# Attention in a macaron block: one exponential per head, and the products with V of two key tiles in a row

## The reference

```
q = (x @ wq.T).reshape(B, S, 16, 16)      # B = 4, S = 2048
k = (x @ wk.T).reshape(B, S, 4, 16)       # 4 key heads, each used by 4 query heads
v = (x @ wv.T).reshape(B, S, 4, 16)
attn = einsum('bqhd,bkhd->bhqk', q, k) / 4
attn = where(causal, attn, -inf)
attn = softmax(attn, axis=-1)
out = einsum('bhqk,bkhd->bqhd', attn, v)
```

## Time and profile before

| | us |
|---|---|
| median of 3 runs (9195.44 to 9199.81) | 9198.21 |
| profiled execution, its own time | 9194.41 |
| its span | 9192.7 |
| exponentials of attention, first start (first call) to last start (second call) | 276.9 to 8605.8 |
| PE busy over the span | 8340.8 (91%) |
| DVE busy | 7658.0 (83%) |
| ACT busy | 4879.4 (53%) |

### The profile page before, as it was taken

One profiled execution on the slowest core, in us unless ns is written; L12 is line 12 of the kernel. 1 busy time (PEld: TensorE's weight loads), 2 busy tenths in 40 slices (PEclk: granted clock), 3 DMA queues, 4 the chain that ended last, 5 costly groups with the idle time before them and its releaser, 6 DMA issues. The chain is left out here.

```text
span 9192.7 us, 130248 instructions
## 1 busy us (share of the span) xinstructions
PE 8340.8 (91%) x35938; PEld 3452.2 (38%) x35938; DVE 7658.0 (83%) x10977; ACT 4879.4 (53%) x7770; POOL 3581.8 (39%) x1746
## 2 busy tenths in 40 slices
PE   7999999999998888888878888888679999999999
PEld 3333333345543333333333333333533333333455
DVE  7888888876666999999979999999278888888666
ACT  3566666642234666665655555555026666666421
POOL 0001000000005999999969999999000000000000
PEclk8899999999999999999989999999879999999999
DMA  6111211122152222222223222222660211111221
GB/s 173 24 25 26 34 25 25 25 51 64 53 192 92 73 68 67 69 66 68 67 88 94 85 87 84 84 87 85 198 156 17 32 26 25 25 25 25 60 64 46
DMA packets 569122, 615.81 MB, mean 67 GB/s; under 512 B 204225, under 2 KB 374209, under 8 KB 568481
## 3 DMA queue, kind: packets, MB, share of 16 engines
q1 hardware_dynamic: 568480, 608.05, 24.7%
HBM read 434.15 MB, written 172.15 MB: 66 GB/s over the span
## 5 line engine op out<-in xcount | busy, mean ns | idle before, releaser
L740 DVE TENSOR_REDUCE ffn_att_mx<-psum 128x1 f32<-128x512 f32 (+3 forms) x4708 | 2909.1, 668 | 541.8 <-PE psum L573 298.7
L697 ACT ACTIVATE ffn_att_e<-psum 128x1024 f32<-128x1024 f32 (+3 forms) x2560 | 2180.8, 895 | 1161.3 <-PE psum L633 1155.7
L570 PE MATMUL psum<-ffn_att_k,ffn_att_q 96*128 96x512 bf16 (+3 forms) x5388 | 1845.1, 361 | 81.0 <-DMA ffn_att_v<-v 76.7
L537 POOL TENSOR_SCALAR_AFFINE_SELECT ffn_att_e<-ffn_att_e 128x512 f32<-128x512 f32 x512 | 324.8, 634 | 3234.6 <-ACT ffn_att_e L697 3234.6
L633 PE MATMUL psum<-ffn_att_q,ffn_att_k 99*128 99x512 bf16 (+3 forms) x5120 | 1500.4, 349 | 27.2 <-issue 26.3
L1517 POOL TENSOR_TENSOR scan_r_h<-scan_r_h,scan_r_cs 128x1024 f32<-128x1024 f32 x512 | 1195.3, 2357 | 202.4 <-ACT scan_r_state L1678 199.1
L1517 POOL TENSOR_TENSOR scan_f_h<-scan_f_h,scan_f_cs 128x1024 f32<-128x1024 f32 x512 | 1193.7, 2357 | 178.9 <-ACT scan_f_state L1678 175.8
L600 PE MATMUL psum<-ffn_att_e,ffn_att_v 128*32 128x512 f32 (+3 forms) x10240 | 1204.0, 542 | 5.1 <-ACT ffn_att_o L716 4.3
L1596 PE MATMUL psum<-scan_f_h,ident 128*128 128x512 f32 x2048 | 1035.0, 647 | 138.6 <-POOL scan_f_h L1517 138.4
L1596 PE MATMUL psum<-scan_r_h,ident 128*128 128x512 f32 x2048 | 997.1, 629 | 126.8 <-POOL scan_r_h L1517 126.0
L570 PEld LDWEIGHTS psum<-ffn_att_k,ffn_att_q 96*128 96x128 bf16 x5388 | 522.0, 98 | 1419.0 <-DVE ffn_att_mx L740 991.1
(11 more groups left out here) (211 smaller groups left out, 8673.6 us busy)
## 6 DMA issues: line engine op xcount, KB each, us to landing
scan_f_cs<-scan_f_bcd SPq DMA_DIRECT2D x264, 256.0 KB, 3.4
scan_r_cs<-scan_r_bcd SPq DMA_DIRECT2D x264, 256.0 KB, 3.4
ffn_att_q<-q_parts SPq DMA_DIRECT2D x72, 384.0 KB, 6.4
q_parts<-ffn_in_q SPq DMA_DIRECT2D x192, 128.0 KB
scan_f_win<-xp SPq DMA_DIRECT2D x18, 1036.0 KB, 7.2
scan_r_win<-xp SPq DMA_DIRECT2D x18, 1036.0 KB, 7.2
ffn_att_q<-q_parts SPq DMA_DIRECT2D x72, 256.0 KB, 8.0
mamba_out_ys<-yz SPq DMA_DIRECT2D x18, 1024.0 KB, 7.0
```

Of the source, the lines that this page charges most:

```text
L570: ins = nc.tensor.matmul(at, q[0:PARTS, i // HALF, h, i % HALF * P:(i % HALF + 1) * P], k[0:PARTS, c * P:c * P + w], start=True, stop=not ...
L697: nc.scalar.activation(E[:, s % PB, 2 * hp:2 * hp + 2, off:CH], psum[:, 2 * hp:2 * hp + 2, off:CH], ACT.Exp, scale=HD ** -0.5).then_inc(e_ ...
L740: nc.vector.reduce_max(mx[:, heads[0]:heads[-1] + 1, i // HALF, i % HALF, c // TT], psum[:, turn, 0:len(heads) * w].rearrange("p (h w) -> ...
```

## The change

1. ACT takes the exponential of one head at a time: four ACTIVATE instructions in a step instead of two, each of half the columns. Each score now has its own semaphore increment and its own wait for the exponential of the same head one step back. The counts on `e_ready` go from 2 to 4 in a step (E0 from 1 to 4).
2. Blocks leave the even steps. Each odd step s does the blocks of steps s - 3 and s - 2 one after the other (`pair_weighted`), between the scores of heads 1 and 2.
3. The pieces of maxima are dealt anew: `room` is 2 widths in an even step and 5 in an odd one (7 in each before). An even step has two slots (after the scores of heads 0 and 2), an odd step five (after the scores of heads 0 and 1, then, behind the pair, after head 2 and twice after head 3).

```diff
-    E0, PV0 = 1, PB - 1
+    E0, PV0 = REP, PB - 1
...
-        room = [7 * width[s] + 400 for s in steps]
+        room = [(5 if s % 2 else 2) * width[s] + 400 for s in steps]
...
                         def score(h):
-                            if h % 2 == 0:
-                                pe.wait_ge(e_ready, E0 + 2 * (it * NB + s) + h // 2 - 1)
-                            ins = nc.tensor.matmul(psum[:, h, off:CH], k[:, kb * P:(kb + 1) * P],
-                                                   q[:, qb * CH // (HALF * P), h, qb * CH % (HALF * P) + off:qb * CH % (HALF * P) + CH], start=True, stop=True)
-                            if h % 2:
-                                ins.then_inc(s_ps, 1)
+                            pe.wait_ge(e_ready, E0 + REP * (it * NB + s - 1) + h + 1)
+                            nc.tensor.matmul(psum[:, h, off:CH], k[:, kb * P:(kb + 1) * P],
+                                                   q[:, qb * CH // (HALF * P), h, qb * CH % (HALF * P) + off:qb * CH % (HALF * P) + CH], start=True, stop=True).then_inc(s_ps, 1)
...
-                        cut = [len(todo) * n // 4 for n in range(5)]
+                        slots = 5 if s % 2 else 2
+                        cut = [-(-len(todo) * n // slots) for n in range(slots + 1)]
...
+                        def pair_weighted():
+                            for z in (s - LAG - 1, s - LAG):
+                                if z >= 0:
+                                    weighted(it, par, z)
+                                elif not first:
+                                    weighted(it - 1, last, NB + z)
                         score(0)
+                        some_maxima(0)
                         score(1)
-                        some_maxima(0)
+                        if s % 2:
+                            some_maxima(1)
+                            pair_weighted()
                         score(2)
-                        some_maxima(1)
+                        some_maxima(2 if s % 2 else 1)
                         score(3)
-                        some_maxima(2)
-                        if s >= LAG:
-                            weighted(it, par, s - LAG)
-                        elif not first:
-                            weighted(it - 1, last, NB + s - LAG)
-                        some_maxima(3)
+                        if s % 2:
+                            some_maxima(3)
+                            some_maxima(4)
...
-                        for hp in range(2):
-                            act.wait_ge(s_ps, 2 * (it * NB + s) + hp + 1)
-                            if hp == 0:
+                        for h in range(REP):
+                            act.wait_ge(s_ps, REP * (it * NB + s) + h + 1)
+                            if h == 0:
                                 act.wait_ge(pv, PV0 + it * NB + s - PB + 1)
-                            nc.scalar.activation(E[:, s % PB, 2 * hp:2 * hp + 2, off:CH], psum[:, 2 * hp:2 * hp + 2, off:CH],
+                            nc.scalar.activation(E[:, s % PB, h, off:CH], psum[:, h, off:CH],
                                                  ACT.Exp, scale=HD ** -0.5).then_inc(e_ready, 1)
```

More of the change, by code:

```diff
@@ L396, in attention @@
     for s in steps:
-        turned.append(turned[-1] + 7 * width[s] + 400)
+        turned.append(turned[-1] + (5 if s % 2 else 2) * width[s] + 400)
     PUTS = 16 * 3
@@ L405, in attention @@
     assert TURN0 + 1 < NB
+    assert NB % 2 == 0 and all(s % 2 for s in range(NB) if closes(s))
     def share(s):
@@ L534, in step @@
                             off = diag(s) * P
-                            hold(pool, e_ready, E0 + 2 * (it * NB + s + 1), pool_passed)
+                            hold(pool, e_ready, E0 + REP * (it * NB + s + 1), pool_passed)
                             part = E[:, s % PB, :, off:off + P]
@@ L592, in weighted @@
                     off = max(diag(s), 0) * P
-                    pe.wait_ge(e_ready, E0 + 2 * (it * NB + s + 1))
+                    pe.wait_ge(e_ready, E0 + REP * (it * NB + s + 1))
                     if diag(s) >= 0:
```

## The result

The changed kernel takes 9251.4 us (median of 4 runs, 9248.2 to 9259.4) against 9198.5 us before: ratio 1.0061, 95% interval 1.0048 to 1.0074. It is 53 us slower. The forecast was 42 us slower, with a range of 9175 to 9290. In the two profiled executions, from which the rows of these two kernels come, the spans differ by 59 us (9251.8 against 9192.7).

What follows compares the result with a forecast made beforehand. PE was taken to bound attention at 104.5 us an iteration; pairs save 5.0, DVE and three banks add 6.3, giving 105.8. The 1.3 us over 32 iterations add 42 to 9198: 9240 us, range 9175 to 9290.

Steps and rivals of the forecast that it cites:

- The bound and the chain: In attention, reduces wait on pieces through three banks; links of 0.74, 0.43 and 0.60 us make eight-piece cycles 5.96 us.
- the sum of its rows: PE's and DVE's starts added up piece by piece for the 20 cycles of an iteration; excesses 6.65 us in all.
- The pair: Two blocks in a row on PE: the second costs its columns alone, saving 0.25 us per pair, 20 pairs an iteration.
- A rule and a row: Second block's weight load: the skill's rule says no saving; the kernel's end, at 256 and 128 columns, showed it overlapping.
- DVE's idle time: At every full-width pair DVE runs out of stored pieces and idles 1.16 us, where before it idled next to nothing.
- The term that was too small: Waiting of PE for DVE through the banks, summed over 20 cycles: 6.3 us an iteration added.
- PE's own work: PE's time for an attention iteration without waits: falls from 104.5 to 99.5 us through 20 pairs.
- the steady part: The attention iterations: 1.3 us longer each, 32 of them costing 42 us.
- The faster one (PE stays the bound): At bank_is_free behind the pair, waits for reduces don't add up: 99.5 us an iteration, 9038 us; chance 0.12.
- Half the excess: Half of the cycles' excess waits is covered: about 102.8 to 104.9 us an iteration, 9144 to 9211 us; chance 0.20.
- The ACT rival: Finer exponentials make ACT late, 3 us an iteration on the path: time about 9340 us; chance 0.03.
- The free seam: Second block's weights don't wait at full width; the rival said they do, 160 us on top, about 9400; chance 0.05.

Runs made afterwards that it cites:

- dealt as before: The changed kernel with the pieces of maxima dealt over the steps with room of 7 widths in every step, as before the change: 9257.0 us.
- The direct comparison: Changed kernel, reduces reading half their columns, plus one slot of maxima moved between a pair's two blocks: 9172.1 us, against 9001 us without that move.
- The kernels with shorter reduces: The changed kernel with each reduce of DVE reading only the first half of its columns: 9001.5 us; the same edit on the kernel before: 9137.2 us.

## Why the prediction was right

**The bound and the chain.** It held step by step. Reduces 0.60 apart, 0.43 from a piece to its reduce, and 0.74 from a reduce to the piece three places on gave 5.96 us for a cycle of eight plain pieces. Measured: 5.96 (dealt as before) and 6.03 with four masks, against the 6.01 that the sum of its rows gives. For the cycle of nine that begins in step 31 the sum gives 6.54, and the last rows show 6.55 (898.87 to 905.42).

**The pair.** A saving of 0.25 us each was forecast. The direct comparison gives 0.27 (5.35 us in 20).

**A rule and a row.** That a second block's weights would have to wait for the first block (the Trainium skill, "TensorE: Matmul & The Clock Gate", Part 3, The mechanism: weight loads overlap matmuls in flight only in other row groups) did not happen. The pair took 1.85 us at full width, just 1.00 + 0.85, with both blocks on all 128 rows. The weight loads of the pair that starts at 898.87 show it in the changed kernel, with the first block's matmuls above them:

```profile
898.87 1.07 PE L601 MATMUL psum<-ffn_att_e,ffn_att_v 128*32 128x512 f32 x8
898.87 0.16 PEld L601 LDWEIGHTS psum<-ffn_att_e,ffn_att_v 128*32 128x32 f32 x8 [0.29 <-issue]
899.32 0.13 PEld L601 LDWEIGHTS psum<-ffn_att_e,ffn_att_v 128*32 128x32 f32 x4 [0.30 <-ACT ffn_att_e L703]
899.75 0.13 PEld L601 LDWEIGHTS psum<-ffn_att_e,ffn_att_v 128*32 128x32 f32 x4 [0.30 <-issue]
```

The profile shows a block as eight loads and eight matmuls (each of the four heads twice), so the eight loads at 898.87 are the first block's, and those at 899.32 belong to the second one already. The first block's matmuls run to 899.94.

**DVE's idle time.** 1.16 us forecast, 1.08 to 1.15 measured in the cycles shown. Over the twelve pairs of two full-width blocks in this iteration it is 0.8 to 1.5 us, so "1.16 in every full-width pair" is right as a middle value only.

**The term that was too small.** Over the 99.5 us of PE's own work 6.3 us an iteration were added, where the 106.53 us need about 7.0. I compared the 20 cycles with the measured ones. Thirteen agree within 0.1 us, and three of those that don't hold the turn of an output. Rows of the changed kernel around one:

```profile
884.72 0.60 PE L609 MATMUL psum<-ident,ffn_att_o 128*128 128x128 f32 x4
885.50 0.25 DVE L767 RECIPROCAL ffn_att_rec<-psum 128x16 f32<-128x16 f32 x1
885.87 0.42 DVE L770 TENSOR_TENSOR ffn_att_on<-psum,ffn_att_rec 128x256 f32<-128x256 f32 x1
886.22 1.28 DVE L746 TENSOR_REDUCE ffn_att_mx<-psum 128x1 f32<-128x512 f32 x2
886.36 0.34 PE L571 MATMUL psum<-ffn_att_k,ffn_att_q 96*128 96x384 bf16 x1
```

I took DVE's part of an output as one more link of the chain with a spacing of 0.72, and gave it the same 0.74 from its start to the piece three places on. But its bank is free only when the second of its two instructions is done, at 886.29. The piece starts at 886.36, which is 0.86 us after 885.50. That is 0.12 too little here, and the three cycles with outputs came out 0.10 to 0.14 above the sum. They make up 0.4 of the missing 0.7 us; where the rest lies is not shown. The kernels with shorter reduces split the 7.0 in another way. The part that goes with the reduces' length is 106.53 - 100.33 = 6.20 us, close to the forecast 6.3. What is left over is 100.33 - 99.5 = 0.83 us that shorter reduces do not remove, and this, not the pair's price, is most of the gap between 4.05 and 5.0 us. The full cycles of eight agree with PE's sum there (5.67 against 5.68). But in two of the four output cycles PE stands some 0.2 us for DVE's two instructions (its pieces at 820.04 and 869.65), and in the one at the start of the iteration 0.19 us for ACT's copy of O (its turn at 859.34). The remainder is not traced.

**From iterations to the whole.** 2.03 us in 32 iterations are 65 us, and 53 were measured (59 between the profiled executions). Most of the difference lies at the ends of the loop body, of which there are four in a call. There PE stands still while nothing that the profile shows holds it, and the granted clock then drops to its lower level (0.5, that is 1.2 instead of 2.4 GHz) for a while: after seven of the eight ends in either kernel, for 3.4 to 10.2 us before and 3.4 us each with the change. Before, in the second call:

```profile
7325.55 0.60 PE L633 MATMUL psum<-ffn_att_q,ffn_att_k 99*128 99x512 bf16 x2 [2.62 <-issue]
7328.26 0.61 PE L633 MATMUL psum<-ffn_att_q,ffn_att_k 99*128 99x512 bf16 x1 [1.89 <-issue]
```

Changed, at the corresponding end:

```profile
7369.78 0.45 PE L633 MATMUL psum<-ffn_att_q,ffn_att_k 99*128 99x512 bf16 x1 [2.09 <-issue]
```

Over both calls these ends cost about 44 us before and 34 us after, so the change was given some 10 us there. The time at the lower clock level alone is 41 us before and 24 after. If PE loses half of that time, which is an estimate from the level of 0.5, it makes 8 of the 10 us. The forecast had no term for this. That 42 came so close to 53 owes something to it: the steady part was 23 us short, and this gave 10 back.

**The rivals.** The faster one (PE stays the bound) needed reduces under 0.53 us. The run with reduces of 420 ns shows that it would have been right in that case. Half the excess needed an iteration of at most 104.9 us, and 106.53 were measured. The ACT rival fell with the table of waits: 7.5 us in 280 for weight loads of scores, which run ahead, and none for PE itself. The free seam is shown above.

## What to carry to other kernels

When work of an in-order queue is gathered into longer uninterrupted runs to save a fixed cost, ask what the consumer of the other work has stored: here three banks of 0.60 us against a run of 2.8 us. The idle time of the consumer (1.1 us) is paid in full as soon as it needs more than the time that is left for the rest, even if its average load is only 86%. And a link in such a chain is as long as the whole holding time of its buffer, all instructions that read it included, not as the consumer's spacing.

## What I had not expected

- One piece between two blocks doesn't relieve DVE at all: the idle time only moves behind the second block (1.06 us), since the store isn't filled again in between.
- In the ends of the loop body, kernels that differ little in attention differ by up to 17 us in the second call: 44 us over both calls before, and about 16 us less in the kernel with one exponential per head, whose iterations take the same time. The granted clock was at its lower level for 10.2 us after the first such end of the second call before, and for 3.4 us after the same one with the finer exponentials; over all ends it was 41 us against 20. Why this is so remains open. The instruction streams differ in length and place, but no run here separates the two.
